# A recommender's interaction kernel: row fetches and product copies change engines, and the last tile is cut into four units

## The chip, the cores and the metric

The kernel runs on one core of one Trainium2 chip. The metric is the device time of one execution in microseconds (us), as a median over runs. All arithmetic is float32.

## The reference

2048 samples are scored. Each has 26 categorical fields; each field looks up a row of 64 numbers in its own table of 12,500 rows. A price gives one more vector of 64. All pairs of the 27 vectors are multiplied (351 products), and a small network follows:

```python
emb = emb_tables[jnp.arange(NUM_FIELDS)[:, None], x_cat]
emb = jnp.transpose(emb, (1, 0, 2))
dense_embed = price[:, None] @ Wp + bp
feats = jnp.concatenate([emb, dense_embed[:, None, :]], axis=1)
gram = jnp.einsum('bid,bjd->bij', feats, feats)
interactions = gram[:, _IU, _JU]
h = jax.nn.relu(dense_embed @ W1 + b1)
dense_out = jax.nn.relu(h @ W2 + b2)
concat = jnp.concatenate([interactions, dense_out], axis=1)
t = jax.nn.relu(concat @ Wt1 + bt1)
out = (t @ Wt2 + bt2)[:, 0]
```

## The kernel before

The samples are worked in 16 tiles of 128. For a tile GpSimd issues one indirect gather for each field (L251): 128 rows of 64 numbers, one for each partition, into `gathered`, of which there is one buffer. The fields stand in two chunks (0 to 13, 14 to 25). A chunk's gathers of the next tile wait until TensorE has transposed that chunk of this tile (`chunk_transposed`). Some columns are fetched without GpSimd: field 25 of nine tiles by SP and field 24 of five tiles by ScalarE, as 128 plain transfers of one row each (L171), whose addresses are first loaded into registers (L168), up to 32 at a time. They land in `pairs_of`, which has room for every such tile, so they can be issued far ahead. ScalarE issues its rows in portions that are written into its program: 26 after a tile's first chunk, 10 after the second and 8 between the two product rounds.

For each chunk TensorE transposes the fields in pairs into `ps_trans` (L500); VectorE copies the even fields and ScalarE the odd ones into `feats` (L196). The products of a tile are 32 matrix products of 128x128 in two rounds of 16 (L540; each is two instructions in the profile, so a round is 32). Both rounds write the same four banks of `ps_gram`, so round 2 waits until round 1 has been copied to `gram` (L186): 16 copies a round, 8 on VectorE and 8 on ScalarE. Tiles are put together into batches of 4, 4, 4, 2, 1 and 1. When a batch's last tile is done, its top layer (L563, L571: two sums of 1 + 7 products, `m` = 0 and 1), relus (ScalarE L339, VectorE L450), score (L579) and store (L344) are worked during the first tile of the next batch. Each engine works its program strictly in the order in which it is written; the waits are on semaphores.

The last tile (15) is laid out in another way: two units of 32 samples for each half of the partitions, with its gathers in four groups (8, 8, 8, 2 columns), four rounds of 8 products over alternating banks, and `keep_warm`, which puts dummy matmuls (L484) into TensorE's waits. Behind the last gather come one transpose, two rounds of products and copies, and the whole top layer of 128 columns.

Of the kernel before, what the change touches and what calls it, by code (L numbers as in the profile page):

```python
# [8 lines left out]
P = 128  # L9
# [6 lines left out]
UNITS = 2  # L16
UNIT = HALF // UNITS
# [9 lines left out]
LAST_CHUNKS = [(0, 8), (8, 16), (16, 24), (24, 26)]  # L27
LAST_ROUNDS = 4
LAST_RG = GROUPS // LAST_ROUNDS

BATCHES = [(0, 4), (4, 8), (8, 12), (12, 14), (14, 15), (15, 16)]
# [4 lines left out]
ACT_TILES = (3, 6, 9, 12, 14)  # L36
# [17 lines left out]
def rec_kernel(nc, price, x_cat, x_rows, table, consts, w1, w2, wt1_pairs, wt1_dense, out):  # L54
# [3 lines left out]
    with ExitStack() as ctx:  # L58
# [12 lines left out]
        last_base = sb("last_base", [P, FIELDS], i32)  # L71
# [65 lines left out]
        top_made = sem("top_made")  # L137
# [9 lines left out]
        last_from = ps_gram[:, :].rearrange("p (r h g s j c) -> p r h g s j c", r=2, h=2, g=LAST_RG, s=GROUP,  # L147
# [30 lines left out]

        def evacuate_gram(copy, t, r, quads):

            n = batch_of[t]
            rg = LAST_RG if t == LAST else RG
            source = last_from[:, r % 2] if t == LAST else gram_from
            for s in quads:
                for c in range(GROUP):
                    last = copy(gram_to[QUAD * c:QUAD * (c + 1), n % 2, t - BATCHES[n][0], :, rg * r:rg * (r + 1), :, s],  # L186
                                source[QUAD * s:QUAD * (s + 1), :, :, s, 0:SLABS, c])
            return last
# [45 lines left out]
        def _(pool):  # L234
# [439 lines left out]
```

## Time and profile before

| | |
|---|---|
| median of 3 runs | 525.37 us (524.44 to 528.44) |
| the profiled execution's own time | 526.02 us |
| its span | 524.1 us |
| GpSimd busy | 381.8 us, 73% of the span |
| TensorE busy (matmul) | 251.3 us, 48% |
| VectorE busy | 148.5 us, 28% |
| ScalarE busy, row fetches not counted | 165.6 us, 32% |
| mean granted TensorE clock | 0.697 of full speed |
| chain that ended last | GpSimd 62%, "issue" 24%, TensorE 5%, DMA 3% |

The issuing of transfers and the register loads are not counted as busy, so ScalarE, which issues 640 row transfers, is more occupied than its share says. A clock of 0.5 is 1.2 GHz and 1.0 is 2.4 GHz.

### The profile page before, as it was taken

Reading aid. Unit: us, or ns where it says so; the run is one execution under the profiler, and the core shown is the slowest. Engines: PE = TensorE matmul, PEld = TensorE weight load, DVE = VectorE, ACT = ScalarE, POOL = GpSimd, SP = SyncE. Lnnn points to the kernel's source line nnn. Section 1 sums busy time; section 2 is a strip of 40 time slices with the busy share of each in tenths; the row PEclk is TensorE's granted clock in tenths of the full one; section 3 lists DMA queues with packets and bytes.
Section 4 is the critical chain, followed back from the end, with each engine's and each line's share of the span. In section 5 each row is a group of like instructions: output and inputs, shape, how many; then the busy total and the mean of one; then the engine's idle time right before and its main releaser. Section 6 shows DMA issues by size and latency. Waiting matters only on the chain.

```text
span 524.1 us, 8045 instructions
## 1 busy us (share of the span) xinstructions
PE 251.3 (48%) x1496; PEld 183.4 (35%) x1496; DVE 148.5 (28%) x370; ACT 165.6 (32%) x405; POOL 381.8 (73%) x411
## 2 busy tenths in 40 slices
PE   0106234151469543443058772606246963467875
PEld 0105124051344323333053351605134333355764
DVE  6103304032240232314033132223324033143353
ACT  0023404133150342405024143332415016164463
POOL 6777777777777777777777777777777777777750
PEclk9999656565569766556566966665555888569798
DMA  6333333333333333233333333333332333332210
GB/s 192 27 28 29 28 29 27 29 28 28 28 29 27 29 28 30 28 28 28 28 30 27 28 29 28 29 29 29 27 29 28 27 30 28 28 29 26 28 22 2
DMA packets 17526, 16.50 MB, mean 31 GB/s; under 512 B 10530, under 2 KB 10786, under 8 KB 17347
## 3 DMA queue, kind: packets, MB, share of 16 engines
q0 software_dynamic: 12864, 13.20, 30.7%
q1 hardware_dynamic: 2884, 2.49, 1.5%
q10 hardware_dynamic: 1728, 0.30, 0.3%
q14 instruction: 38, 0.31, 0.2%
q8 instruction: 12, 0.20, 0.1%
HBM read 15.95 MB, written 0.01 MB: 30 GB/s over the span
## 4 chain that ended last, share of the span: by engine, by line
POOL 62%; issue 24%; PE 5%; DMA 3%; ACTq 2%; ACT 2%; DVE 0%; POOLq 0%
POOL gathered L251 61%; PE ps_mlp L571 3%; ACTq L171 2%; POOL pairs_of L251 2%; DMA gathered<-in_table,row_idx 2%; ACT gram L186 1%; PE ps_trans L500 1%; PE ps_gram L540 1%; DMA pairs_of<-in_table,row_idx 1%; PE ps_mlp L563 1%; ACTq L168 0%; DMA raw_idx<-in_x_cat 0%; POOLq L58 0%; ACT scores L344 0%; ACT top L339 0%
## 5 line engine op out<-in xcount | busy, mean ns | idle before, releaser
L251 POOL DMA_INDIRECT gathered<-in_table,row_idx x390 | 369.3, 947 | 120.4 <-issue 116.9
L540 PE MATMUL ps_gram<-feats 64*128 64x128 f32 x1024 | 111.9, 402 | 87.2 <-ACT gram L186 56.3
L540 PEld LDWEIGHTS ps_gram<-feats 64*128 64x128 f32 x1024 | 104.3, 306 | 101.5 <-issue 86.4
L186 DVE COPY gram<-ps_gram 32x112 f32<-32x112 f32 (+1 forms) x272 | 93.4, 343 | 152.8 <-PE ps_gram L540 149.6
L186 ACT COPY gram<-ps_gram 32x112 f32<-32x112 f32 (+1 forms) x272 | 93.7, 345 | 128.0 <-PE ps_gram L540 87.4
L500 PE MATMUL ps_trans<-ident,gathered 128*128 128x128 f32 x195 | 41.2, 368 | 173.9 <-DMA pairs_of<-in_table,row_idx 97.1
L500 PEld LDWEIGHTS ps_trans<-ident,gathered 128*128 128x128 f32 x195 | 31.0, 190 | 187.8 <-issue 186.3
L196 ACT COPY feats<-ps_trans 64x448 f32<-64x448 f32 (+1 forms) x60 | 34.1, 568 | 167.3 <-PE ps_trans L500 109.9
L196 DVE COPY feats<-ps_trans 64x448 f32<-64x448 f32 (+1 forms) x60 | 36.5, 609 | 148.9 <-PE ps_trans L500 148.3
L571 PE MATMUL ps_mlp<-gram,wt1p_sb 128*128 128x512 f32 (+2 forms) x168 | 60.8, 523 | 4.6 <-ACT gram L186 4.6
L571 PEld LDWEIGHTS ps_mlp<-gram,wt1p_sb 128*128 128x128 f32 x168 | 32.7, 229 | 33.7 <-issue 27.2
L450 DVE TENSOR_SCALAR top<-ps_mlp,consts_sb 128x512 f32<-128x512 f32 (+2 forms) x6 | 3.4, 573 | 65.4 <-PE ps_mlp L571 65.4
L289 ACT ACTIVATE feats<-price_bc,consts_sb 64x64 f32<-64x64 f32 x32 | 15.6, 488 | 0.7
L251 POOL DMA_INDIRECT pairs_of<-in_table,row_idx x12 | 11.3, 944 | 3.7 <-issue 3.7
L563 PE MATMUL ps_mlp<-dense_out,wt1d_sb 64*128 64x512 f32 (+2 forms) x24 | 12.5, 609 | 2.0 <-ACT dense_out L334 2.0
L339 ACT ACTIVATE top<-ps_mlp,consts_sb 128x512 f32<-128x512 f32 (+2 forms) x6 | 3.3, 545 | 26.2 <-PE ps_mlp L571 26.2
L196 ACT ACT_TABLE_LOAD x1 | 1.3, 1283 | 25.2 <-issue 25.2
L579 PE MATMUL ps_mlp<-top,consts_sb 128*1 128x512 f32 (+2 forms) x24 | 7.8, 449 | 1.0 <-DVE top L450 1.0
L530 PE MATMUL ps_mlp<-hidden,w_sb 128*64 128x512 f32 (+2 forms) x12 | 7.6, 728 | 0.5 <-ACT hidden L329 0.5
L563 PEld LDWEIGHTS ps_mlp<-dense_out,wt1d_sb 64*128 64x128 f32 x24 | 4.4, 227 | 6.3 <-issue 4.1
L525 PE MATMUL ps_mlp<-dense,w_sb 64*128 64x512 f32 (+2 forms) x12 | 5.8, 573 | 1.5 <-ACT scores L344 1.5
L484 PE MATMUL ps_trans<-wt1p_sb,ident 128*128 128x256 f32 x24 | 6.1, 389 | 0.0
(31 smaller groups left out, 52.4 us busy)
## 6 DMA issues: line engine op xcount, KB each, us to landing
pairs_of<-in_table SPq DMA_DIRECT2D x1152, 0.2 KB
pairs_of<-in_table ACTq DMA_DIRECT2D x640, 0.2 KB
gathered<-in_table,row_idx POOLq DMA_INDIRECT x390, 3.3
price_bc<-in_price SPq DMA_DIRECT2D x1, 1024.0 KB, 7.1
wt1p_sb<-in_wt_pairs SPq DMA_DIRECT2D x1, 896.0 KB, 9.2
raw_idx<-in_x_cat SPq DMA_DIRECT2D x1, 195.0 KB, 2.6
pairs_of<-in_table,row_idx POOLq DMA_INDIRECT x12, 3.3
w_sb<-in_w ACTq DMA_DIRECT2D x2, 32.0 KB, 4.0
```

The costliest lines, as they stand in the source:

```text
L171: eng.dma_start(field_at(t, f, 1)[p0 + k:p0 + k + 1, :].bitcast(u8), table_bytes[:, bass.ds(row, ROW_BYTES)])\
L186: last = copy(gram_to[QUAD * c:QUAD * (c + 1), n % 2, t - BATCHES[n][0], :, rg * r:rg * (r + 1), :, s], source[QUAD * s:QUAD * (s + 1), :, ...
L196: last = copy(feats[D * h:D * (h + 1), :, 1 + f0 + q:f1 + q:2], src[D * q:D * (q + 1), h, :, :])
L251: pool.indirect_dma_start(out=field_at(t, f, 1), out_offset=None, in_=rows, in_offset=bass.IndirectOffsetOnAxis(ap=row_idx[:, at:at + 1], ...
L289: return nc.scalar.activation(dst, price_bc[part, first:first + n], ACT.Identity, bias=const(BP, part), scale=const(WP, part))
L484: nc.tensor.matmul(ps_trans[:, BANK * bank:BANK * bank + TM1], ident[:, :], wt1p_sb[:, 0:TM1], start=True, stop=True)
L500: last = nc.tensor.transpose(ps_trans[:, to + k * P:to + (k + 1) * P], field_at(t, f, 2), ident[:, :])
L530: nc.tensor.matmul(ps_mlp[1][0:BM2, 0:width(n)], w2_sb[:, :], hidden[:, 0:width(n)], start=True, stop=True)\
L540: last = nc.tensor.matmul(ps_gram[:, out_at:out_at + P], group, group, start=True, stop=True)
L563: nc.tensor.matmul(ps_mlp[m][:, 0:w], wt1d_sb[:, m * P:(m + 1) * P], dense_out[:, 0:w], start=True, stop=False)
L571: last = nc.tensor.matmul(ps_mlp[m][:, 0:w], wt1p_sb[:, j * TM1 + m * P:j * TM1 + (m + 1) * P], gram[:, at:at + w], start=False, stop=(j = ...
L579: last = nc.tensor.matmul(ps_mlp[0][0:1, 0:width(n)], const(WT2 + m), top[m][:, 0:width(n)], start=(m == 0), stop=(m == 1))
```

## The change

ScalarE now fetches field 24 of seven tiles row by row instead of five (896 rows, in portions of 28 and 36 for each tile). For that, the product copies of tiles 0 to 13 are all VectorE's, 16 a round. The small network of the price (`hidden_layer`, `dense_out_layer`) is worked in the first four tiles for all samples. The batches are 4, 4, 4, 2 and 2 tiles, so the top layer of tile 14 is not worked alone. Tile 14's products go in four rounds of 8 over alternating banks, and both engines copy them.

The last tile is gathered in four units of 32 samples (7, 6, 7 and 6 columns); each unit has its own transposes, copies and one round of 8 products. The top layer of the last batch is split: 160 columns (tile 14 and unit 0) are summed around unit 1's products, the other 96 (units 1 to 3) at the end, in `ps_trans`. The output leaves in two transfers, all but the last 96 scores first. The row indices of the last tile are made by twelve small adds on VectorE instead of one. The dummy matmuls are now four before unit 3's transposes and four before the late top sums.

```diff
-UNITS = 2
-UNIT = HALF // UNITS
+UNITS = 4
+UNIT = P // UNITS
...
-BATCHES = [(0, 4), (4, 8), (8, 12), (12, 14), (14, 15), (15, 16)]
+BATCHES = [(0, 4), (4, 8), (8, 12), (12, 14), (14, 16)]
...
-ACT_TILES = (3, 6, 9, 12, 14)
+ACT_TILES = (2, 4, 6, 8, 10, 12, 14)
...
-FIRST_ROWS, AFTER_FIRST_CHUNK, AFTER_CHUNKS, BETWEEN_ROUNDS = 24, 26, 10, 8
+FIRST_ROWS, AFTER_FIRST_CHUNK, AFTER_CHUNKS = 24, 28, 36
...
-WARM = (0, 7, 3, 1, 1)
-TO_GRAM, TO_TOP = 4, 5
+WARM = (0, 0, 4, 4)
...
+            for late in range(2):
+                part = slice(BATCH - LATE, BATCH) if late else slice(0, BATCH - LATE)
+                sp.wait_ge(score_stored, len(BATCHES) + late)
+                sp.dma_start(out.rearrange("(o b) -> o b", o=1)[:, part], scores[:, part]).then_inc(out_written, 16)
...
             def gram_round(r, t):
-                dve.wait_ge(gram_done, ROUNDS * t + r + 1)
-                evacuate_gram(nc.vector.tensor_copy, t, r, (0, 1)).then_inc(gram_evac_dve, 1)
+                dve.wait_ge(gram_done, rounds_before(t) + r + 1)
+                evacuate_gram(nc.vector.tensor_copy, t, r, range(GROUP) if t < LAST - 1 else (0, 1)).then_inc(gram_evac_dve, 1)
...
-            t, n = LAST, batch_of[LAST]
-            even_last(0)
-            top_relu(n - 1)
-            even_last(1)
-            for r in range(LAST_ROUNDS // 2):
-                gram_round(r, t)
-            even_last(2)
-            even_last(3)
-            for r in range(LAST_ROUNDS // 2, LAST_ROUNDS):
-                gram_round(r, t)
-            top_relu(n)
+            t = LAST
+            for n in range(UNITS):
+                even_unit(n)
+                gram_round(n, t)
+                if n == 1:
+                    part_relu(0)
+            part_relu(1)
...
+            for n in range(UNITS):
+                transpose_unit(n)
+                if n == 1:
+                    top_part(0, 0)
+                fine_round(LAST, n)
+                if n == 1:
+                    top_part(1, 0)
+                if n == 2:
+                    score_part(0)
+            keep_warm(UNITS, 0)
+            for m in range(2):
+                top_part(m, 1)
+            score_part(1)
```

ScalarE's program from the top relu of the batch of tiles 8 to 11, in tile 12. `pairs_of<-in_table` are the row fetches, `x26` that many of them. Before:

```order
L339 ACTIVATE top<-ps_mlp,consts_sb 128x512 [waits top_summed0]
L168 TENSOR_LOAD by_row_at
L171 DMA pairs_of<-in_table 1x256 x26
L196 COPY feats<-ps_trans 64x64x6 [waits chunk_transposed1]
L196 COPY feats<-ps_trans 64x64x6
L344 ACTIVATE scores<-ps_mlp,consts_sb 1x512 [waits score_summed]
L168 TENSOR_LOAD by_row_at
L171 DMA pairs_of<-in_table 1x256 x10
L186 COPY gram<-ps_gram 32x2x8x7 [waits gram_done]
L186 COPY gram<-ps_gram 32x2x8x7 x7
```

And now:

```order
L368 ACTIVATE top<-ps_mlp,consts_sb 128x512 [waits top_summed0]
L175 TENSOR_LOAD by_row_at
L178 DMA pairs_of<-in_table 1x256 x28
L212 COPY feats<-ps_trans 64x64x6 [waits chunk_transposed1]
L212 COPY feats<-ps_trans 64x64x6
L378 ACTIVATE scores<-ps_mlp,consts_sb 1x512 [waits score_summed]
L175 TENSOR_LOAD by_row_at
L178 DMA pairs_of<-in_table 1x256 x32
L175 TENSOR_LOAD by_row_at
L178 DMA pairs_of<-in_table 1x256 x4
```

The 16 product copies of the tile are gone, and the fetches that stood around them follow the second chunk's copies in one piece of 32 + 4 rows; the portion behind the top relu has grown from 26 to 28 rows, with the odd copies of the second chunk still behind it.

VectorE's program in tile 13, before:

```order
L196 COPY feats<-ps_trans 64x64x7 [waits chunk_transposed0]
L196 COPY feats<-ps_trans 64x64x7
L196 COPY feats<-ps_trans 64x64x6 [waits chunk_transposed1]
L196 COPY feats<-ps_trans 64x64x6
L186 COPY gram<-ps_gram 32x2x8x7 [waits gram_done]
L186 COPY gram<-ps_gram 32x2x8x7 x7
L186 COPY gram<-ps_gram 32x2x8x7 [waits gram_done]
L186 COPY gram<-ps_gram 32x2x8x7 x7
```

And now:

```order
L212 COPY feats<-ps_trans 64x64x7 [waits chunk_transposed0]
L212 COPY feats<-ps_trans 64x64x7
L212 COPY feats<-ps_trans 64x64x6 [waits chunk_transposed1]
L212 COPY feats<-ps_trans 64x64x6
L203 COPY gram<-ps_gram 32x2x8x7 [waits gram_done]
L203 COPY gram<-ps_gram 32x2x8x7 x15
L203 COPY gram<-ps_gram 32x2x8x7 [waits gram_done]
L203 COPY gram<-ps_gram 32x2x8x7 x15
```

Each round has 16 copies for 8; the second round of products, which writes the same banks, can only follow the sixteenth copy.

TensorE's end, from the dummies before the last group's transposes. Before:

```order
L484 MATMUL ps_trans<-wt1p_sb,ident 128x256 [waits trans_evac_act,trans_evac_dve]
L484 MATMUL ps_trans<-wt1p_sb,ident 128x256 x2
L500 MATMUL ps_trans<-ident,gathered 128x128 [waits last_gathered3]
L484 MATMUL ps_trans<-wt1p_sb,ident 128x256 [waits trans_evac_act,trans_evac_dve]
L540 MATMUL ps_gram<-feats 128x128 [waits gram_evac_dve,dense_slot_set,gram_evac_act,trans_evac_act,trans_evac_dve]
L540 MATMUL ps_gram<-feats 128x128 x7
L540 MATMUL ps_gram<-feats 128x128 [waits gram_evac_dve,dense_slot_set,gram_evac_act,trans_evac_act,trans_evac_dve]
L540 MATMUL ps_gram<-feats 128x128 x7
L563 MATMUL ps_mlp<-dense_out,wt1d_sb 128x128 [waits dense_out_made]
L484 MATMUL ps_trans<-wt1p_sb,ident 128x256
L571 MATMUL ps_mlp<-gram,wt1p_sb 128x128 [waits gram_evac_act,gram_evac_dve]
```

And now:

```order
L536 MATMUL ps_trans<-wt1p_sb,ident 128x256 [waits trans_evac_act,trans_evac_dve]
L536 MATMUL ps_trans<-wt1p_sb,ident 128x256 x3
L574 MATMUL ps_trans<-ident,gathered 128x128 [waits unit_gathered3]
L574 MATMUL ps_trans<-ident,gathered 128x128 x2
L621 MATMUL ps_gram<-feats 128x128 [waits gram_evac_dve,dense_slot_set,gram_evac_act,trans_evac_act,trans_evac_dve]
L621 MATMUL ps_gram<-feats 128x128 x7
L536 MATMUL ps_trans<-wt1p_sb,ident 128x256 x4
L627 MATMUL ps_trans<-dense_out,wt1d_sb 128x96
L632 MATMUL ps_trans<-gram,wt1p_sb 128x96 [waits gram_evac_act,gram_evac_dve]
L632 MATMUL ps_trans<-gram,wt1p_sb 128x96 x6
L627 MATMUL ps_trans<-dense_out,wt1d_sb 128x96
L632 MATMUL ps_trans<-gram,wt1p_sb 128x96 [waits gram_evac_act,gram_evac_dve]
```

One round of products stands behind the last transposes instead of two, and the top sums behind it are 96 columns wide instead of 128.

## Rows read from the trace of the kernel before

**Rows 1.** Page part 5: costliest groups of instructions, GpSimd's gathers.

```profile
L251 POOL DMA_INDIRECT gathered<-in_table,row_idx x390 | 369.3, 947 | 120.4 <-issue 116.9
...
L251 POOL DMA_INDIRECT pairs_of<-in_table,row_idx x12 | 11.3, 944 | 3.7 <-issue 3.7
```

**Rows 2.** Timeline of the tail (start us, us, engine line op names shapes xcount [idle before]).

```profile
505.90 0.94 POOL L251 DMA_INDIRECT gathered<-in_table,row_idx  x1 [0.31 <-issue]
...
508.71 0.33 PE L500 MATMUL ps_trans<-ident,gathered 128*128 128x128 f32 x1 [0.60 <-DMA gathered<-in_table,row_idx]
...
509.72 2.06 PE L540 MATMUL ps_gram<-feats 64*128 64x128 f32 x32 [0.24 <-DVE feats L211]
...
510.92 4.29 DVE L186 COPY gram<-ps_gram 32x56 f32<-32x56 f32 x16 [1.30 <-PE ps_gram L540]
...
515.36 2.83 PE L571 MATMUL ps_mlp<-gram,wt1p_sb 128*128 128x128 f32 x14 [2.76 <-ACT gram L186]
...
518.83 2.04 PE L571 MATMUL ps_mlp<-gram,wt1p_sb 128*128 128x128 f32 x14
...
521.96 0.36 ACT L344 ACTIVATE scores<-ps_mlp,consts_sb 1x128 f32<-1x128 f32 x1 [3.37 <-PE ps_mlp L579]
```

**Rows 3.** Timeline of ScalarE, tile 7 at 247, tile 12 from 414, tile 13 at 452.

```profile
247.29 1.26 ACT L196 COPY feats<-ps_trans 64x448 f32<-64x448 f32 x2 [1.67 <-PE ps_trans L500]
...
249.51 8.59 ACTq L171 DMA_DIRECT2D pairs_of<-in_table  x26
...
414.17 0.69 ACT L339 ACTIVATE top<-ps_mlp,consts_sb 128x512 f32<-128x512 f32 x1 [7.59 <-PE ps_mlp L571]
...
425.48 1.03 ACT L196 COPY feats<-ps_trans 64x384 f32<-64x384 f32 x2 [10.62 <-issue]
...
428.00 3.45 ACTq L171 DMA_DIRECT2D pairs_of<-in_table  x10
...
452.18 1.03 ACT L196 COPY feats<-ps_trans 64x384 f32<-64x384 f32 x2 [8.38 <-issue]
```

**Rows 4.** Timeline of VectorE and GpSimd in the opening, and one gather at 392.

```profile
6.99 0.18 DVE L428 TENSOR_TENSOR row_idx<-clamped,last_base 128x26 uint32<-128x26 f32 x1
...
9.53 1.42 POOL L251 DMA_INDIRECT gathered<-in_table,row_idx  x1 [0.30 <-issue]
...
392.27 0.94 POOL L251 DMA_INDIRECT gathered<-in_table,row_idx  x1 [0.31 <-issue]
```

**Rows 5.** SP's timeline; and line 168, register loads, ns min/median/max.

```profile
7.40 457.20 SPq L171 DMA_DIRECT2D pairs_of<-in_table  x1152
...
L168 ACTq TENSOR_LOAD <-by_row_at x47: 483/2094/2430, 15.1 to 459.3; - x47
```

**Rows 6.** Timeline of VectorE and TensorE, second chunk and products of tile 11.

```profile
386.30 1.21 DVE L196 COPY feats<-ps_trans 64x384 f32<-64x384 f32 x2 [12.56 <-PE ps_trans L500]
...
387.56 3.78 PE L540 MATMUL ps_gram<-feats 64*128 64x128 f32 x32 [1.30 <-DVE feats L196]
...
391.39 2.84 DVE L186 COPY gram<-ps_gram 32x112 f32<-32x112 f32 x8 [3.88 <-PE ps_gram L540]
```

**Rows 7.** Timeline of TensorE's top sums in tiles 12 and 14, VectorE's copies then.

```profile
405.67 8.45 PE L571 MATMUL ps_mlp<-gram,wt1p_sb 128*128 128x512 f32 x14
...
468.28 4.86 PE L571 MATMUL ps_mlp<-gram,wt1p_sb 128*128 128x256 f32 x14 [1.81 <-ACT gram L186]
...
473.70 3.29 PE L571 MATMUL ps_mlp<-gram,wt1p_sb 128*128 128x256 f32 x14
...
477.77 1.21 DVE L196 COPY feats<-ps_trans 64x384 f32<-64x384 f32 x2 [0.26 <-PE ps_trans L500]
```

**Rows 8.** Groups by line and shape, window 464 to 530, VectorE's copies.

```profile
L186 DVE COPY gram<-ps_gram 32x56 f32<-32x56 f32 x32 | 8.2, 255 | 4.8 <-PE ps_gram L540 4.3
...
L211 DVE COPY feats<-ps_trans 64x192 f32<-64x192 f32 x2 | 1.0, 484 | 0.1
```

**Rows 9.** TensorE by stretch: us, busy (xcount), granted clock, DMA share, GB/s.

```profile
515.00:518.00 3.00, 2.65 (x14) 0.65 0.00 0
```

More of the change, by code:

```diff
@@ L15 @@
 HALF = P // 2
-UNITS = 2
-UNIT = HALF // UNITS
+UNITS = 4
+UNIT = P // UNITS
+SIDE = UNIT // 2
+COLS = FIELDS // UNITS
+SHARED = UNITS * COLS
 GROUPS = HALF // GROUP
@@ L136, in rec_kernel @@
         top_summed = [sem(f"top_summed{m}") for m in range(2)]
-        top_made = sem("top_made")
+        top_made = [sem(f"top_made{m}") for m in range(2)]
         score_summed = sem("score_summed")
@@ new lines, in top_sums @@
+            def top_sums(n, m, part, to, rounds):
+                a, first = BATCHES[n][0] * P, (n % 2) * SLABS * WIDE * P
+                nc.tensor.matmul(to, wt1d_sb[:, m * P:(m + 1) * P], dense_out[:, a + part.start:a + part.stop],
+                                 start=True, stop=False)
+                wait_gram_evac(rounds)
+                for j in range(SLABS):
+                    at = first + j * WIDE * P
+                    last = nc.tensor.matmul(to, wt1p_sb[:, j * TM1 + m * P:j * TM1 + (m + 1) * P],
+                                            gram[:, at + part.start:at + part.stop], start=False, stop=(j == SLABS - 1))
+                last.then_inc(top_summed[m], 1)
@@ L575, in score, with top_part @@
+            def top_part(m, late):
+                if not late:
+                    pe.wait_ge(score_stored, last_batch)
+                top_sums(last_batch, m, *last_part(m, late), rounds_before(LAST) + (FINE_ROUNDS if late else 1))
             def score(n):
-                pe.wait_ge(top_made, 2 * n + 2)
                 for m in range(2):
+                    pe.wait_ge(top_made[m], n + 1)
                     last = nc.tensor.matmul(ps_mlp[0][0:1, 0:width(n)], const(WT2 + m), top[m][:, 0:width(n)],
+                                            start=(m == 0), stop=(m == 1))
+                last.then_inc(score_summed, 1)
@@ L580, in score, with score_part @@
+            def score_part(late):
+                part, _ = last_part(0, late)
+                for m in range(2):
+                    pe.wait_ge(top_made[m], last_batch + 1 + late)
+                    last = nc.tensor.matmul(ps_mlp[late][0:1, 0:part.stop - part.start], const(WT2 + m), top[m][:, part],
                                             start=(m == 0), stop=(m == 1))
@@ L651 @@
     idx = cat.transpose(2, 1, 0).copy()
-    idx[:, -1] = cat[:, -1].reshape(FIELDS // 2, 2, 2, UNITS, UNIT).transpose(1, 2, 4, 3, 0).reshape(P, FIELDS)
+    last = cat[:, -1].reshape(FIELDS, UNITS, 2, SIDE)
+    own = last[:SHARED].reshape(COLS, UNITS, UNITS, 2, SIDE).transpose(1, 3, 4, 2, 0).reshape(P, UNITS, COLS)
+    shared = last[SHARED:].reshape(2, 2, 2, 2, SIDE).transpose(2, 0, 3, 4, 1).reshape(P, 2)
+    for n in range(UNITS):
+        idx[:, -1, UNIT_COLS[n][0]:UNIT_COLS[n][0] + COLS] = own[:, n]
+        if n % 2 == 0:
+            idx[:, -1, UNIT_COLS[n][COLS]] = shared[:, n // 2]
     idx = idx.reshape(P, TILES * FIELDS)
```

344 lines of the change are left out of this document (191 added, 153 removed).

## Prediction

> **What bounds the kernel now.** I read the page's costliest groups first. GpSimd issues 390 + 12 = 402 gathers of 0.94 us with 0.30 us between them, almost nothing of it a wait for another engine [rows 1]: one gather every 1.25 us, up to the last one at 505.90 us. Behind it stands a tail of 18.2 us to the span's end at 524.1: landing 2.8 us, transposes, copies, products, 4.29 us of product copies, the two top sums, score, store and the output [rows 2]. So there are two ways to gain: fewer gathers, or a shorter tail. Everything else has been hidden, and I then read how well: the timeline of the three compute engines around tiles 11 to 14, and ScalarE's row fetches in it.
>
> There the cover is thin. ScalarE does its row fetches between its copies, and the copies wait behind them: at tile 12 it takes the top sum at 414.17 and reaches the odd copies of the second chunk only at 425.48, and those of tile 13 at 452.18 [rows 3]. TensorE's products wait for these copies.
>
> **The change, part by part.** *Gathers.* 16 of 416 columns are fetched row by row instead of 14: 400 gathers, 2 x 1.25 = 2.5 us earlier at the end (by tile 11 both are already gone, so tiles 11 to 15 arrive 2.5 us earlier).
>
> *Opening.* Twelve small adds on VectorE take the place of one of 0.18 us, and its row addresses are 14% longer; beside such work a gather takes up to 1.42 us instead of 0.94, 0.34 us lost for each us of it [rows 4]. With some 2.3 us more of it the bounds are 0 and 0.8 us; I take 0.35, since most opening gathers lose less than that slowest one. Last gather: 505.90 - 2.5 + 0.35 = 503.8.
>
> *ScalarE.* It loses 16 product copies per tile and gets 28 + 36 rows per tile for 26 + 10 + 8. From the start of its copies to the end of 26 rows it needs (249.51 + 8.59) - 247.29 = 10.8 us [rows 3]; 28 rows: 11.5. SP, whose 1152 rows are 36 pieces of 32, needs 457.2 / 36 = 12.7 us for each [rows 5]; the 36 are a piece of 32 and one of 4, 12.7 + 2.1 (0.48 for the shortest register load, 4 x 0.34, gaps) = 14.8; with the gaps a tile costs ScalarE about 26.9 us. A tile is 24 to 26 gathers, 30 to 32.5 us. It fits, but in a batch's first tile ScalarE first waits for the top sum and then fetches 28 rows.
>
> *VectorE.* 16 copies of 0.355 us instead of 8 beside ScalarE: 5.7 us a round for 2.84 to 3.2, with ScalarE no longer late for the round. TensorE's second round waits for it, so a tile's products take 2 x (3.8 + 5.7) = 19 us [rows 6].
>
> Now the path. Tile 8 is a batch's first tile like tile 12, 100 gathers or 125 us ahead of it: its odd copies start near 425.5 - 125 = 300.5 now, and about then after the change (two rows more, but an earlier arrival); three tiles of 26.9 bring ScalarE to tile 11's at 381.2, before the transposes, 386.30 - 2.5 = 383.8 [rows 6]. Products: 383.8 + 1.3 + 3.8 + 5.7 + 3.9 + 5.7 = 404.2. Top sum of tiles 8 to 11: 8.45 [rows 7], to 412.8. ScalarE to the odd copies of tile 12: 11.3 + 0.7 = 12.0, to 424.8. From there 14.8 of rows, or products 1.1 + 3.4 + 5.7 + 3.5 and the next transposes, 1.3: both about 440. 28 rows: 451.5, tile 13's odd copies. That is where they are now (452.18), though the gathers came 2.5 us earlier: **the two saved gathers are gone in ScalarE's queue.** Products and copies of tile 13: 1.1 + 3.9 + 5.7 + 3.8 + 5.7, to 471.7, where the top sum now starts at 468.28: VectorE's longer copies cost another 3.5 us. First sum 5.3 (4.86 now, 6.0 wholly at 1.2 GHz), second 0.6 + 3.3, transposes 0.9: tile 14's last copies start at 481.9 instead of 477.77 [rows 7].
>
> *Last tiles*, with the shapes of [rows 2] and [rows 8]. Tile 14 in four rounds: 1.3 + 1.2, then 4 x 2.15 (half of 4.29) of copies on both engines: 493.0. Unit 0: dense slots 1.0, copies 1.0, products 1.3, copies 2.15: 498.4. Unit 1 and the early top sums: 160 columns are not in the trace; 14 instructions lie between 2.04 (128 columns) and 3.29 (256), I take 2.3. First sum 500.9, products 502.2, second sum 504.9. Unit 2: transposes 0.7, VectorE two copies of the shared columns (64 elements; 56 take 0.26) and two of 0.48, 1.5, products 1.3: 508.4, copied at 510.5; TensorE does the score and four dummies (8 instructions of 256 columns at 3.29 / 14 = 0.235 [rows 7], 1.9) to 510.9. Unit 3, landed since 503.8 + 2.8 = 506.6: transposes 511.5, copies 512.5, products 513.8, copied 515.9, first late sum (96 columns; at most 2.04, at least three quarters of it, 1.5; take 1.8) 517.9, second 520.2, relu, score, store 521.4, output 1.8: 523.2. TensorE is idle in half of this stretch. Its granted clock fell to 0.65 on average in the stretch after the last wait of now [rows 9], and fourteen instructions took 2.83 instead of 2.04 [rows 2]; I add 2.0 (bounds 0 and 4). **Span 525.2, 1.1 more than 524.1.**
>
> The Trainium skill speaks against this change here (TensorE: Matmul & The Clock Gate, "HAM oscillation"): short bursts of matmuls with idle time between them fall back to the half clock each time. By that rule the end would stand at the bound of 4 us, a span of 527.2, and by [rows 9], where part of such a stretch ran at full clock, at 2.
>
> The profiled execution has 526.02 us for its span of 524.1, 0.65 above the median of three. I apply the difference to the median: 525.37 + 1.1 = **526.5 us**.
>
> **Rivals.** *Nothing is late.* ScalarE is through its rows before each second chunk, and unit 3 is taken when it lands: transposes 507.2 instead of 511.5, 4.3 less, and the clock's 2.0 shrinks to 1: span 519.9 to 518.9, time 520.1 to 521.1. For it: the tail alone is really shorter, one round of copies behind the last gather instead of two (2.15), 96 columns for 128, and the output of the rest already gone. Against it: ScalarE at 452.18 today, with 8 rows fewer a tile 13. Chance 0.14. This is about the most that the change can give: 1%.
>
> *ScalarE does not catch up* (the other side). The 10 rows behind the second chunk's copies come 2.5 us after these started (425.48 to 428.00 [rows 3]), as late as 26 rows behind their copies (247.29 to 249.51), though the shortest load takes 0.48 [rows 5]; if the 36 carry such a surcharge, or a row takes 0.36, a tile costs 28.8. It decides from (383.8 - 300.5) / 3 = 27.8 us a tile: above it ScalarE is still late at tile 12, and again at 13. At 28.8: 3 us late at tile 8, 5.4 at tile 11, 7.5 at tile 13's odd copies, and TensorE's transposes then hold up GpSimd too (their slack is eleven gathers, 13.7 us, less some 5 for landing and transposes). Span 525.2 + 7.5 = 532.7, time 534. Chance 0.16.
>
> *VectorE's copying slows the gathers.* At the opening's 0.34 us for each us, 28 rounds x 2.84 = 80 us more copying would cost up to 27 us, a span of 552. But the gather at 392.27, beside the product copies that began at 391.39, takes 0.94 us [rows 4, 6]. Chance 0.02. The Trainium skill (SBUF — State Buffer, "Who interferes with whom") says why both can be: a VectorE instruction with two SBUF inputs holds up a GpSimd one that reads SBUF, and fp32 copies from SBUF to SBUF starve the gathers, but with one SBUF input at most and outside the two-port modes there is no contention; by its warning on copies alone this change would be slower, by its condition not, and the trace agrees with the condition.
>
> **How the numbers follow.** Forecast 0.63 (524 to 529), nothing late 0.14 (half of it just beyond 1%), ScalarE late 0.16, gathers slowed 0.02; the other 0.05 are smaller mishaps within 1%. A measurement of this kernel tells about 1% from no change, 520.1 and 530.6: faster 0.09, within 0.73, slower 0.18. Range 520.5 to 532, which leaves half of the first rival and most of the slow ones out. The forecast's own range is 524 to 529.
>
> **What would show it.** 400 gathers every 1.25 us, the last started near 503.8. ScalarE's odd copies of tile 13 near 451 and its rows ending just before; gaps of TensorE in front of them. The top sum of tiles 12 and 13 starting near 472. Unit 3's transposes near 511 rather than 507; if they stand at 507, the chain through ScalarE was not late. A GpSimd wait on transposes around tiles 9, 13 or 14 would show the slow rival. A gather over 1.0 us in mid-kernel would show shared ports.

## The result and the profile after

The changed kernel takes 529.2 us (median of 20 runs, 527.0 to 531.3), the kernel before 526.18 us (20 runs, 524.44 to 528.53): ratio 1.0057, 95% interval 1.0043 to 1.0071, 0.6% slower. The forecast was 526.5 us against 525.37, a ratio of 1.0022, most likely within 1%. The profiled execution of the changed kernel has 530.84 us and a span of 528.9 us, that of before 526.02 and 524.1. The spans below stand 1.8 to 2.1 us under the times; the profiled execution after is at the upper end of its runs.

GpSimd in the page's costliest groups, then the slowest gather of the opening, the two gathers ahead of which it waits for TensorE, and the last one (start us, us, engine line op names xcount [idle before]); they answer to [rows 1, 2]:

```profile
L274 POOL DMA_INDIRECT gathered<-in_table,row_idx x394 | 373.9, 949 | 124.3 <-issue 118.4
```

```profile
12.60 1.56 POOL L274 DMA_INDIRECT gathered<-in_table,row_idx  x1 [0.30 <-issue]
...
195.09 0.94 POOL L274 DMA_INDIRECT gathered<-in_table,row_idx  x1 [0.94 <-PE ps_trans L553]
...
321.56 0.94 POOL L274 DMA_INDIRECT gathered<-in_table,row_idx  x1 [1.85 <-PE ps_trans L553]
...
506.36 0.94 POOL L274 DMA_INDIRECT gathered<-in_table,row_idx  x1 [0.30 <-issue]
```

Two gathers are gone, 2.5 us, and yet the last one starts at 506.36, later than the 505.90 of [rows 2]. Eight slow gathers of the opening cost 2.06 us over 0.95 where seven cost 1.31 before, 0.75 more; the slowest of them, 1.56 us, is slower than the 1.42 of [rows 4]. The two waits cost 0.64 and 1.55 us beyond the usual 0.30. 505.90 - 2.5 + 0.75 + 2.19 = 506.34.

ScalarE's timeline in tiles 12 and 13, for [rows 3]:

```profile
416.77 0.69 ACT L368 ACTIVATE top<-ps_mlp,consts_sb 128x512 f32<-128x512 f32 x1 [9.97 <-PE ps_mlp L632]
419.04 9.38 ACTq L178 DMA_DIRECT2D pairs_of<-in_table  x28
428.47 1.03 ACT L212 COPY feats<-ps_trans 64x384 f32<-64x384 f32 x2 [11.01 <-issue]
...
430.79 13.10 ACTq L178 DMA_DIRECT2D pairs_of<-in_table  x36
...
446.17 9.58 ACTq L178 DMA_DIRECT2D pairs_of<-in_table  x28
455.79 1.03 ACT L212 COPY feats<-ps_trans 64x384 f32<-64x384 f32 x2 [9.33 <-issue]
```

The odd copies of the second chunk come at 428.47 in tile 12 (425.48 before) and at 455.79 in tile 13 (452.18 before), each time the moment the 28 rows are issued. The chain that ended last shows who waited (start us, us, what; "issue" is a wait that it can't put down to an engine). In the kernel before, this chain ran along the gathers up to 505.90 [rows 2]; now it leaves them in tile 11:

```profile
381.49 3.85 DMA pairs_of<-in_table,row_idx
385.58 1.53 PE ps_trans L553 x6
388.70 3.80 PE ps_gram L600 x32
398.42 3.80 PE ps_gram L600 x32
408.07 8.66 PE ps_mlp L632 x14
...
426.45 3.15 issue
429.60 3.49 PE ps_gram L600 x32
439.01 3.80 PE ps_gram L600 x32
449.96 1.55 PE ps_trans L553 x6
452.72 4.20 issue
456.92 3.80 PE ps_gram L600 x32
466.64 3.80 PE ps_gram L600 x32
476.30 5.68 PE ps_mlp L632 x14
```

The two "issue" pieces, 3.15 and 4.20 us, are TensorE waiting with the transposes done, until ScalarE is through its rows. VectorE's sixteen copies lie between the rounds:

```profile
392.52 5.75 DVE L203 COPY gram<-ps_gram 32x112 f32<-32x112 f32 x16 [4.21 <-PE ps_gram L600]
```

5.75 us, twice the 2.84 of [rows 6]. The top sum of tiles 12 and 13 starts at 476.30, where [rows 7] has 468.28. TensorE's timeline of the last tile, for [rows 2]:

```profile
499.62 2.08 PE L621 MATMUL ps_gram<-feats 64*128 64x128 f32 x16 [4.30 <-ACT feats L222]
...
503.97 4.07 PE L632 MATMUL ps_mlp<-gram,wt1p_sb 128*128 128x160 f32 x14 [0.61 <-DVE gram L198]
...
509.56 2.17 PE L632 MATMUL ps_mlp<-gram,wt1p_sb 128*128 128x160 f32 x14
...
513.75 1.16 PE L621 MATMUL ps_gram<-feats 64*128 64x128 f32 x16 [1.59 <-DVE feats L222]
...
517.31 0.49 PE L574 MATMUL ps_trans<-ident,gathered 128*128 128x128 f32 x3
...
522.45 1.77 PE L632 MATMUL ps_trans<-gram,wt1p_sb 128*128 128x96 f32 x14
...
524.54 1.80 PE L632 MATMUL ps_trans<-gram,wt1p_sb 128*128 128x96 f32 x14
```

Unit 3's transposes begin at 517.31. Its last gather started at 506.36 and landed near 509, so they come 8 us later than they could: no work of this tail waits for GpSimd any more. The clock by stretch (us, TensorE busy, granted clock, DMA share, GB/s), for [rows 9]:

```profile
500.00:508.00 8.00, 7.39 (x37) 0.50 0.14 27
...
515.00:518.00 3.00, 2.80 (x15) 1.00 0.00 0
520.00:528.00 8.00, 6.86 (x46) 1.00 0.01 2
```

### The profile page after: what moved, and what is told of

Read it like the earlier page. It is cut to its first block, busy times and chain, and to the rows that moved or that the text cites. A ratio compares the mean times of both kernels' runs of the same rounds, so it can differ in the third digit from the quotient of the medians.

```text
span 528.9 us, 8560 instructions
## 1 busy us (share of the span) xinstructions
PE 252.3 (48%) x1481; PEld 184.7 (35%) x1481; DVE 229.1 (43%) x623; ACT 86.5 (16%) x189; POOL 380.3 (72%) x407
## 4 chain that ended last, share of the span: by engine, by line
POOL 34%; PE 28%; issue 18%; DVE 15%; DMA 3%; ACT 2%; POOLq 0%
POOL gathered L274 34%; DVE gram L203 13%; PE ps_mlp L632 11%; PE ps_gram L600 9%; PE ps_trans L553 2%; DMA pairs_of<-in_table,row_idx 2%; ACT gram L200 2%; DVE feats L212 1%; PE ps_gram L621 1%; PE ps_mlp L653 1%; DMA gathered<-in_table,row_idx 1%; PE ps_mlp L627 1%; PE ps_trans L536 1%; PE ps_trans L632 1%; DVE gram L198 0%
## 5 line engine op out<-in xcount | busy, mean ns | idle before, releaser
L274 POOL DMA_INDIRECT gathered<-in_table,row_idx x394 | 373.9, 949 | 124.3 <-issue 118.4
L203 DVE COPY gram<-ps_gram 32x112 f32<-32x112 f32 x448 | 155.8, 348 | 146.3 <-PE ps_gram L600 136.7
L600 PE MATMUL ps_gram<-feats 64*128 64x128 f32 x896 | 104.6, 419 | 121.8 <-DVE gram L203 83.1
L553 PE MATMUL ps_trans<-ident,gathered 128*128 128x128 f32 x184 | 38.7, 369 | 131.5 <-DMA gathered<-in_table,row_idx 70.3
L500 DVE TENSOR_SCALAR top<-ps_mlp,consts_sb 128x512 f32<-128x512 f32 (+1 forms) x4 | 2.7, 684 | 52.3 <-PE ps_mlp L632 52.3
L621 PE MATMUL ps_gram<-feats 64*128 64x128 f32 x128 | 10.2, 305 | 9.9 <-ACT feats L222 4.3
L198 DVE COPY gram<-ps_gram 32x56 f32<-32x56 f32 x32 | 8.2, 257 | 10.2 <-PE ps_gram L621 9.9
L363 ACT ACTIVATE dense_out<-ps_mlp,consts_sb 64x512 f32<-64x512 f32 x4 | 2.7, 682 | 59.0 <-PE ps_mlp L590 29.6
L198 ACT COPY gram<-ps_gram 32x56 f32<-32x56 f32 x32 | 8.3, 259 | 6.6 <-PE ps_gram L621 6.2
L200 DVE COPY gram<-ps_gram 32x56 f32<-32x56 f32 x32 | 8.0, 251 | 1.7 <-PE ps_gram L621 1.3
L368 ACT ACTIVATE top<-ps_mlp,consts_sb 128x512 f32<-128x512 f32 (+1 forms) x4 | 2.5, 634 | 36.5 <-PE ps_mlp L632 36.5
L200 ACT COPY gram<-ps_gram 32x56 f32<-32x56 f32 x32 | 8.1, 253 | 1.4 <-PE ps_gram L621 1.0
L584 PE MATMUL ps_mlp<-dense,w_sb 64*128 64x512 f32 x8 | 8.3, 1137 | 0.0
```

The source lines that it names most:

```text
L198: last = copy(gram_unit[to, w, k, r, :, :, :, s], fine_from[part, r % 2, :, :, s, 0:SLABS, c])
L200: last = copy(gram_to[to, w, k, :, FINE_RG * r:FINE_RG * (r + 1), :, s], fine_from[part, r % 2, :, :, s, 0:SLABS, c])
L203: last = copy(gram_to[to, w, k, :, RG * r:RG * (r + 1), :, s], gram_from[part, :, :, s, 0:SLABS, c])
L274: pool.indirect_dma_start(out=field_at(t, f, 1), out_offset=None, in_=rows, in_offset=bass.IndirectOffsetOnAxis(ap=row_idx[:, at:at + 1], ...
L553: last = nc.tensor.transpose(ps_trans[:, to + k * P:to + (k + 1) * P], field_at(t, f, 2), ident[:, :])
L584: nc.tensor.matmul(ps_mlp[0][:, :], w1_sb[:, :], dense[:, :], start=True, stop=True).then_inc(hidden_summed, 1)
```

## The experiments

Twelve runs of seven kernels. Each edit is made in the changed kernel. The runs fell on five chips, always beside the kernel before, so ratios are compared, and spans only with care. On two of the chips every kernel, the one before too, takes at least 340 us more; what these runs can say stands at the end of this section. The theory was that ScalarE's queue sets the pace in tiles 12 and 13; the rivals were VectorE's long rounds and the last tile's own work.

**The old tiles 0 to 13 under the new last tiles.** The product copies are shared again, and ScalarE fetches five tiles in the old portions.

```diff
-ACT_TILES = (2, 4, 6, 8, 10, 12, 14)
+ACT_TILES = (3, 6, 9, 12, 14)
...
-FIRST_ROWS, AFTER_FIRST_CHUNK, AFTER_CHUNKS = 24, 28, 36
+FIRST_ROWS, AFTER_FIRST_CHUNK, AFTER_CHUNKS, BETWEEN_ROUNDS = 24, 26, 10, 8
...
-                evacuate_gram(nc.vector.tensor_copy, t, r, range(GROUP) if t < LAST - 1 else (0, 1)).then_inc(gram_evac_dve, 1)
+                evacuate_gram(nc.vector.tensor_copy, t, r, (0, 1)).then_inc(gram_evac_dve, 1)
```

> The changed kernel's last two tiles, opening, batches and dense network, but with tiles 0 to 13 as before: product copies split 8 and 8 between the engines, ScalarE fetches five tiles in portions of 24, 26, 10 and 8 rows, 402 gathers. Theory (tiles 0 to 13 lose the time, the last tile in units gains some): last gather 505.90 + 0.75 of the opening = 506.7, top sum of tiles 12 and 13 near 468, tile 14's last copies near 478, unit 3's transposes right behind its landing, about 510.5, and from there the 11.6 us of the changed kernel (517.31 to 528.9): span about 522, ratio to the kernel before about 0.996. Rival (the units themselves cost more than the old tail): span 526 or more, ratio above 1.003.

Measured: 523.89 us beside 527.07, ratio 0.9938 (0.9915 to 0.996), span 522.7; the last gather started at 507.26, and TensorE's timeline has

```profile
468.43 4.95 PE L635 MATMUL ps_mlp<-gram,wt1p_sb 128*128 128x256 f32 x14 [1.17 <-ACT gram L203]
...
511.02 0.49 PE L577 MATMUL ps_trans<-ident,gathered 128*128 128x128 f32 x3
```

As the theory had it (468, 510.5, 522). The rest of the change taken together (the last two tiles, the early top sums, the batches, the network in the first four tiles) is a gain of 0.6%; the run doesn't part these from one another. The last gather is 1.36 us behind the 505.90 of [rows 2], but not for the reason expected: six slow gathers of this opening cost 1.38 us over 0.95, hardly more than before, and the gathers of this run start 1.2515 us apart instead of 1.2487. The changed tiles 0 to 13 turn the gain into a loss: 1.0057 - 0.9938 = 0.0119, 6.3 us.

**Five tiles for ScalarE instead of seven, VectorE still copying alone.** This cuts those 6.3 us in two.

```diff
-ACT_TILES = (2, 4, 6, 8, 10, 12, 14)
+ACT_TILES = (3, 6, 9, 12, 14)
...
-FIRST_ROWS, AFTER_FIRST_CHUNK, AFTER_CHUNKS = 24, 28, 36
+FIRST_ROWS, AFTER_FIRST_CHUNK, AFTER_CHUNKS = 24, 20, 24
```

> The changed kernel, but ScalarE fetches five tiles instead of seven (3, 6, 9, 12, 14) in portions of 24, 20 and 24 rows: 402 gathers, 44 rows a tile instead of 64; all product copies of tiles 0 to 13 stay VectorE's. Against the kernel with the old tiles 0 to 13 (span 522.7, five tiles too, copies split 8 and 8) it shows what VectorE's sixteen copies cost, against the changed kernel (528.9) what the two more tiles cost. Theory (most of the loss is ScalarE's rows): 20 rows behind the top relu, odd copies of tile 12 near 424; second chunk of tile 13 at its transposes near 449.5, products 3.8 + 5.75 + 3.8 + 5.75, top sum near 470 instead of 468.43 (old tiles) and 476.30 (changed kernel); span about 524.3, ratio to the kernel before 0.997. Rival (VectorE's long rounds are the loss): top sum at 474 or later, span 527 or more, ratio 1.003 or more.

Measured: 523.43 us beside 526.12, ratio 0.9952 (0.9933 to 0.997), span 521.7. ScalarE in tiles 12 and 13, and TensorE's top sum:

```profile
424.16 1.03 ACT L212 COPY feats<-ps_trans 64x384 f32<-64x384 f32 x2 [7.58 <-PE ps_trans L553]
...
448.68 1.03 ACT L212 COPY feats<-ps_trans 64x384 f32<-64x384 f32 x2 [7.37 <-PE ps_trans L553]
```

```profile
469.10 5.51 PE L632 MATMUL ps_mlp<-gram,wt1p_sb 128*128 128x256 f32 x14 [2.82 <-DVE gram L203]
```

Both odd copies now wait for transposes and not for rows, and the top sum comes at 469.10, 0.7 us behind the kernel with shared copies, whose gathers were late by themselves (the last one at 507.26, here at 506.13). So with five tiles VectorE's sixteen copies cost 0.9952 - 0.9938 = 0.0014, less than the intervals; beside these copies the two more tiles of rows cost 1.0057 - 0.9952 = 0.0105, 5.5 us, although they save two gathers. This settles it between rows and rounds. Seven tiles with shared copies were not run, so what the long rounds add once ScalarE is late isn't shown.

**The rows in another place.** Nothing is left out: in the tiles 4, 8, 12 and 14 the 28 rows are issued while ScalarE would wait for the top sum, and not behind it.

```diff
+                fetch_some(AFTER_FIRST_CHUNK)
                 if first:
                     top_relu(n - 1)
-                fetch_some(AFTER_FIRST_CHUNK)
                 odd_fields(1, t)
```

> The changed kernel with one edit: in the tiles 4, 8, 12 and 14 ScalarE issues the 28 rows ahead of the top relu, in the 10 us in which it now waits for the top sum (406.8 to 416.77 in tile 12), instead of behind it. Theory (the end is set by a chain through ScalarE's queue): the odd copies of tile 12's second chunk come at about 425 instead of 428.47, right behind TensorE's transposes (424.6); the two waits of GpSimd at 195 and 321 (0.94 and 1.85 us) vanish, last gather near 504.2; the chain from tile 12 on shifts by 3.6 us: span about 525.3 instead of 528.9, ratio to the kernel before about 0.999. Rival (VectorE's doubled copies, not the rows, hold the chain): the odd copies move, the products do not start earlier, ratio stays 1.006.

Measured: 524.5 us beside 525.46, ratio 0.9981 (0.9965 to 0.9997), span 523.2, with

```profile
413.99 0.69 ACT L368 ACTIVATE top<-ps_mlp,consts_sb 128x512 f32<-128x512 f32 x1 [9.53 <-PE ps_mlp L632]
421.90 1.03 ACT L212 COPY feats<-ps_trans 64x384 f32<-64x384 f32 x2 [7.22 <-PE ps_trans L553]
```

No gather waits for TensorE beyond the usual 0.30 us any more, and the last one starts at 504.18 (504.2 was expected). The shift was undersized: the odd copies of tile 12 come 6.6 us earlier, 3.8 of it between the top relu and them (7.9 instead of 11.7), and 2.8 because the top relu itself comes earlier; 2.2 of these are the gathers' two waits. One line of order is worth 1.0057 - 0.9981 = 0.0076, 4.0 us. The tail is still late: in tile 13 the odd copies wait for 28 rows until 450.54, and unit 3's transposes come at 511.53, over 7 us behind the start of the last gather.

**Rows ahead, none in tile 13, and tile 13's copies shared.** Beside the edit above:

```diff
-                fetch_some(AFTER_CHUNKS)
-                if t == LAST - 1:
-                    for r in range(FINE_ROUNDS):
+                fetch_some(AFTER_CHUNKS + (4 if t < 10 else 0))
+                if t >= LAST - 2:
+                    for r in range(ROUNDS if t < LAST - 1 else FINE_ROUNDS):
...
-                evacuate_gram(nc.vector.tensor_copy, t, r, range(GROUP) if t < LAST - 1 else (0, 1)).then_inc(gram_evac_dve, 1)
+                evacuate_gram(nc.vector.tensor_copy, t, r, range(GROUP) if t < LAST - 2 else (0, 1)).then_inc(gram_evac_dve, 1)
```

> The changed kernel with three edits in ScalarE's and VectorE's programs: the 28 rows ahead of the top relu in the tiles 4, 8, 12 and 14; 40 rows instead of 36 behind the second chunk of tiles 0 to 9, so that tile 13 has none; and the product copies of tile 13 shared by both engines, 8 and 8. 400 gathers as before. Theory (the change's loss lies in the rows and long copies of tiles 12 and 13 alone): odd copies of tile 12 near 425, of tile 13 near 448 instead of 455.79, top sum of tiles 12 and 13 at 463 to 465 instead of 476.30, tile 14's last copies near 475, last gather near 504.2, unit 3's transposes right behind its landing near 507.2, then 11.7 us: span about 519, ratio to the kernel before about 0.987. Rival (the gathers of tile 14 are held up by transposes elsewhere, or four rows more a tile make ScalarE late from the first tiles): span 522.7 or more, no better than the kernel with the old tiles 0 to 13.

Measured: 520.44 us beside 525.46, ratio 0.9913 (0.9886 to 0.994), span 518.4. TensorE's timeline:

```profile
465.41 5.09 PE L632 MATMUL ps_mlp<-gram,wt1p_sb 128*128 128x256 f32 x14
...
506.65 0.55 PE L574 MATMUL ps_trans<-ident,gathered 128*128 128x128 f32 x3 [1.21 <-DMA gathered<-in_table,row_idx]
```

The last transposes wait for the landing again, 2.5 us behind the last gather's start at 504.13, and from there it is 11.75 us to the end. This is faster than both kernels, by 0.9% against the one before, and it is the prediction's rival "nothing is late" (518.9 to 519.9) brought about. Against the kernel with the rows ahead it gains 0.9981 - 0.9913 = 0.0068, 3.6 us; how much of this is the rows that tile 13 no longer has, and how much its shared copies, was not measured.

**The dummies and the clock.** These runs fell on the two slow chips, whose times don't compare; but their last 20 us, in which no row is fetched, have the same durations as elsewhere: from the start of unit 2's products to the end of the span the changed kernel needs 528.9 - 513.75 = 15.15 us, and the kernel with the rows ahead on such a chip 868.8 - 853.65 = 15.15. That stretch is compared.

```diff
-WARM = (0, 0, 4, 4)
+WARM = (0, 0, 0, 4)
```

> The changed kernel without the four dummy products ahead of unit 3's transposes (1.99 us from 515.48), where unit 3 has landed long before. Theory (they lie on the path now that TensorE is late, and only pay if the clock would fall without them): transposes 1.8 us earlier, unit 3's products at most 0.9 us longer (1.16 against 2.08), the last dummies stay: span 0.9 to 1.8 us shorter. Rival (the granted clock falls for the late top sums too): the two sums and products take 1.88 times as long, 3.9 us more, span 2 us longer.

Measured: ratio 1.0051 (1.0025 to 1.0077); the stretch is 867.5 - 851.01 = 16.5 us, 1.3 us longer. The transposes came at once:

```profile
852.74 0.55 PE L574 MATMUL ps_trans<-ident,gathered 128*128 128x128 f32 x3
855.96 1.83 PE L621 MATMUL ps_gram<-feats 64*128 64x128 f32 x16 [2.67 <-DVE feats L222]
857.72 2.95 PE L536 MATMUL ps_trans<-wt1p_sb,ident 128*128 128x256 f32 x8
```

ScalarE's timeline at the same place:

```profile
852.22 2.24 ACT L198 COPY gram<-ps_gram 32x56 f32<-32x56 f32 x8 [1.79 <-PE ps_gram L621]
...
854.89 0.97 ACT L222 COPY feats<-ps_trans 64x192 f32<-64x192 f32 x2
```

The theory, a gain of 0.9 to 1.8 us, failed in two points. The four dummies are hardly on the path: ScalarE copies unit 2's products until 854.46 and takes unit 3's features only then, so the 1.8 us gained on TensorE become 0.2 at unit 3's products (4.95 us behind the start of unit 2's instead of 5.16). And without them the products (1.83 for 1.16) and the next dummies (2.95 for 1.99) run in part at the half clock. The late sums did not (1.80 each), which the rival had wanted.

In the kernel "late tiles", all dummies away, `WARM = (0, 0, 0, 0)`:

> The kernel with ScalarE's rows ahead of the top relu, none in tile 13 and that tile's product copies shared (span 518.4, unit 3's transposes right behind their landing at 506.65), now without the eight dummy products, which there lie wholly beside waits for the landing and for the last product copies. Theory (the dummies hold the granted clock at 1.0 in the last stretch): unit 3's products 2.08 instead of 1.16 us, the two late sums 3.3 each instead of 1.77 and 1.80, their two first products 0.9 longer: span 3 to 4.8 us longer, 521.4 to 523.2. Rival (unit 2's and unit 3's own work holds the clock): span within 0.5 us of 518.4.

Measured: ratio 1.0171 (1.014 to 1.0202), and in the stretch

```profile
877.41 3.27 PE L632 MATMUL ps_trans<-gram,wt1p_sb 128*128 128x96 f32 x14 [2.08 <-DVE gram L198]
...
881.28 3.30 PE L632 MATMUL ps_trans<-gram,wt1p_sb 128*128 128x96 f32 x14
```

887.3 - 868.41 = 18.9 us, 3.7 more than with the dummies; the granted clock from 872 to 887 was 0.56, against 1.00 in the kernel with the rows ahead from 854 to 868. The eight dummies are worth 3.7 us at this end, as the theory had it (3 to 4.8); by the run above, 1.3 of them are those of the first four. The rest of the ratio, about 9 us over the others there, lies ahead of this stretch; the kernel "late tiles" with its dummies was not run on that chip, so its cause stays open.

Eight dummies more between unit 0's transposes and products, in the idle time of 4.3 us there:

```diff
-WARM = (0, 0, 4, 4)
+WARM = (8, 0, 4, 4)
...
-                keep_warm(n, n % 2)
+                if n > 1:
+                    keep_warm(n, n % 2)
...
+                if n == 0:
+                    keep_warm(1, 1)
```

> The changed kernel with eight dummy products more, on TensorE between unit 0's transposes and its products, where it is idle from 495.3 to 499.6 (4.3 us; four of them take 1.99 us at 1.0). Theory (the half clock in unit 0's products and the first early top sum costs time on the path): the products take 1.16 instead of 2.08 us, the fourteen instructions of 160 columns 2.2 instead of 4.07, span 2.0 to 2.8 us shorter, about 526.5. Rival (the chain behind it is set by the copies, or the dummies run at half clock and delay the products): no change, or up to 4 us longer.

The second run had the same expectation, the third one more number:

> The changed kernel with eight dummy products more, on TensorE between unit 0's transposes and its products, where it is idle from 495.3 to 499.6 (4.3 us; four of them take 1.99 us at 1.0). Theory (the half clock in unit 0's products and the first early top sum costs time on the path): the products take 1.16 instead of 2.08 us, the fourteen instructions of 160 columns 2.2 instead of 4.07, span 2.0 to 2.8 us shorter, about 526.5. Rival (the chain behind it is set by the copies, or the dummies run at half clock and delay the products): no change, or up to 4 us longer.

> The changed kernel with eight dummy products more, on TensorE between unit 0's transposes and its products, where it is idle from 495.3 to 499.6 (4.3 us; four of them take 1.99 us at 1.0). Theory (the half clock in unit 0's products and the first early top sum costs time on the path): the products take 1.16 instead of 2.08 us, the fourteen instructions of 160 columns 2.2 instead of 4.07, and the stretch from the start of unit 0's products to that of unit 2's 11.2 us instead of 14.13; span 2.0 to 2.8 us shorter, about 526.5. Rival (the chain behind it is set by the copies, or the dummies run at half clock and delay the products): no change, or up to 4 us longer.

It ran three times, each time on a slow chip: ratios 1.0014 (0.999 to 1.0038), 1.0026 (0.9996 to 1.0055) and 1.003 (1.0002 to 1.0058). From the start of unit 0's products to unit 2's it took 13.97, 11.17 and 13.64 us, against 14.13 in the changed kernel. In the second the products and the first early sum ran at the high level:

```profile
839.11 4.43 PE L536 MATMUL ps_trans<-wt1p_sb,ident 128*128 128x256 f32 x10 [0.60 <-issue]
845.52 1.16 PE L622 MATMUL ps_gram<-feats 64*128 64x128 f32 x16 [1.98 <-ACT feats L222]
...
849.06 2.14 PE L633 MATMUL ps_mlp<-gram,wt1p_sb 128*128 128x160 f32 x14 [1.44 <-ACT gram L198]
```

The dummies did not hold the clock there: it was granted at 0.50 from 839 to 843.5, so they ran at the half level themselves, and at 1.00 from 845.5 on. In the other two runs the products took 2.08 us, at 0.50. In the third the dummies were as long (ten instructions in 4.57 us at 0.50), with 3.44 us of idle time behind them in place of 1.98, and the clock did not rise. In the first the clock was 1.00 from 829 to 832, 0.59 beside the last five dummy instructions, and 0.50 in the 3.75 us of idle time behind them. So the half clock costs 14.13 - 11.17 = 3.0 us in this stretch. These dummies removed it in one run of three, and why in that one stays open. None of the three shows what eight would do in the 4.3 us of the other chips: here TensorE had over 12 us between unit 0's transposes and its products, and the dummies lay scattered in them.

**The slow chips.** The first runs of the kernels with the old tiles, with the rows ahead and with five tiles fell on them. Their expectations were those of the second runs, but for the rival of the rows ahead:

> The changed kernel's last two tiles, opening, batches and dense network, but with tiles 0 to 13 as before: product copies split 8 and 8 between the engines, ScalarE fetches five tiles in portions of 24, 26, 10 and 8 rows, 402 gathers. Theory (tiles 0 to 13 lose the time, the last tile in units gains some): last gather 505.90 + 0.75 of the opening = 506.7, top sum of tiles 12 and 13 near 468, tile 14's last copies near 478, unit 3's transposes right behind its landing, about 510.5, and from there the 11.6 us of the changed kernel (517.31 to 528.9): span about 522, ratio to the kernel before about 0.996. Rival (the units themselves cost more than the old tail): span 526 or more, ratio above 1.003.

> The changed kernel with one edit: in the tiles 4, 8, 12 and 14 ScalarE issues the 28 rows ahead of the top relu, in the 10 us in which it now waits for the top sum (406.8 to 416.77 in tile 12), instead of behind it. Theory (the end is set by a chain through ScalarE's queue): the odd copies of tile 12's second chunk come at about 425 instead of 428.47, right behind TensorE's transposes (424.6); the two waits of GpSimd at 195 and 321 (0.94 and 1.85 us) vanish, last gather near 504.2; the chain from tile 12 on shifts by 3.6 us: span about 525.3 instead of 528.9, ratio to the kernel before about 0.999. Rival (the last tile's own work is too long, whatever comes ahead of it): the odd copies move, the end does not, ratio stays 1.006.

> The changed kernel, but ScalarE fetches five tiles instead of seven (3, 6, 9, 12, 14) in portions of 24, 20 and 24 rows: 402 gathers, 44 rows a tile instead of 64; all product copies of tiles 0 to 13 stay VectorE's. Against the kernel with the old tiles 0 to 13 (span 522.7, five tiles too, copies split 8 and 8) it shows what VectorE's sixteen copies cost, against the changed kernel (528.9) what the two more tiles cost. Theory (most of the loss is ScalarE's rows): 20 rows behind the top relu, odd copies of tile 12 near 424; second chunk of tile 13 at its transposes near 449.5, products 3.8 + 5.75 + 3.8 + 5.75, top sum near 470 instead of 468.43 (old tiles) and 476.30 (changed kernel); span about 524.3, ratio to the kernel before 0.997. Rival (VectorE's long rounds are the loss): top sum at 474 or later, span 527 or more, ratio 1.003 or more.

None of the forecast places can be read there, since the ends are set elsewhere. Measured: 866.82 us (ratio 0.9987, 0.9963 to 1.0011), 870.3 (1.0053, 1.0027 to 1.0079) and 875.4 (1.001, 0.9989 to 1.0032), beside 866.37, 866.37 and 874.88 for the kernel before. SP's and ScalarE's timelines of the first:

```profile
7.41 800.73 SPq L178 DMA_DIRECT2D pairs_of<-in_table  x1152
```

```profile
399.54 24.56 ACTq L178 DMA_DIRECT2D pairs_of<-in_table  x13
```

SP's 1152 transfers take 800.73 us there, 457.20 in [rows 5], and thirteen of ScalarE's 24.56 us instead of some 5. The chain that ended last is 60% SP's queue, so GpSimd's gathers, which bound the kernel elsewhere, don't there.

## Why the prediction held, and where it was off

By its own steps, in the spans of the two profiled executions:

| Step | forecast | measured |
|---|---|---|
| last gather starts | 503.8 | 506.36 |
| products of tile 11 start | 385.1 | 388.70 |
| odd copies, second chunk of tile 12 | 424.8 | 428.47 |
| the same of tile 13 | 451.5 | 455.79 |
| top sum of tiles 12 and 13 starts | 471.7 | 476.30 |
| tile 14's last feature copies | 481.9 | 486.51 |
| unit 0's copies start | 493.0 | 497.52 |
| first early sum ends | 500.9 | 508.04 |
| unit 3's transposes end | 511.5 | 517.80 |
| end of the span | 525.2 | 528.9 |

**Right: the mechanism and the sign of the tail.** The two saved gathers are gone in ScalarE's queue; the odd copies of tile 13 wait for its 28 rows; the last transposes come long after their landing; VectorE's round takes 5.75 us (5.7 forecast) and slows no gather in mid-kernel. The run with five tiles shows that the rows are the main cause, and the one with the rows ahead that their place is. From tile 11 to tile 14 the forecast's intervals hold within 0.6 us: 39.7 from tile 11's products to tile 12's odd copies (39.8 measured), 26.7 to tile 13's (27.3), 20.2 to the top sum (20.5), 10.2 to tile 14's copies (10.2), 11.1 to the units (11.0).

**Off: the arrival.** The step "its odd copies start near 300.5 now, and about then after the change" failed. Before the change they do (300.16); after it they come at 305.14:

```profile
284.21 9.14 PE L632 MATMUL ps_mlp<-gram,wt1p_sb 128*128 128x512 f32 x14 [1.30 <-DVE gram L203]
...
305.14 1.03 ACT L212 COPY feats<-ps_trans 64x384 f32<-64x384 f32 x2 [11.06 <-issue]
```

Of these 5.0 us, 2.0 are there before the top sum: TensorE transposes tile 8's first chunk at 279.19 instead of 277.20. The sum then waited 1.30 us for VectorE's copies of tile 7 (the forecast counted the long rounds in tile 11, but not there), and it took 9.14 us for 7.71, at a granted clock of 0.68 for 0.81. The 28 rows that follow the relu add only 0.2 to what 26 took; but they stand behind it, so its lateness reaches the copies in full. Behind the batches' first tiles, 4 and 8, TensorE's first transposes of tiles 5 and 9 came so late that the gathers of tiles 6 and 10, which wait for them, stood 0.64 and 1.55 us. That the rows behind the relu are their cause is shown by the run with the rows ahead, which has neither wait. The forecast had this only in its rival "ScalarE does not catch up", at 0.16 and with 7.5 us. What happened is a light form of it: late in the batches' first tiles, caught up by the fourth (in tile 11 ScalarE ends its rows 0.4 us behind the transposes), and the 2.2 us stayed in the gathers. The opening cost 0.75 us instead of 0.35, because the slowest gather beside VectorE was not the one of [rows 4]; and the forecast left its 0.35 out where it put tile 11's transposes at 386.30 - 2.5. Together this is 2.9 of the 3.6 us by which tile 11's products are late. The last gather of tile 11 took 0.4 us longer to the transposes (4.09 from its start for 3.71), and the odd copies began at 387.57, 0.4 us behind VectorE's at 387.13.

**Off: where the clock falls.** The forecast put 2.0 us for the half clock behind unit 2, by [rows 9]. It fell earlier, in unit 0's products and the first early sum: 2.08 and 4.07 us for the 1.3 and 2.3 taken, 2.6 us, and none behind unit 2, where the granted clock is 1.00 and the dummies hold it. The sizes came to nearly the same, the place did not. The Trainium skill's rule (TensorE: Matmul & The Clock Gate, "HAM oscillation") is that short bursts of matmuls with idle time between them fall back to the half clock. By the prediction's own reading it would have brought 4 us. The run without dummies (3.7 us) and the 3.0 us in units 0 and 1 agree with it; the end of the changed kernel doesn't test it, since dummies fill the idle time there.

**Off: the end.** From the end of unit 3's transposes it took 11.1 us for a forecast of 13.7, which had the 2.0 of the clock in it. This error hid a part of the others: the changed kernel was 3.6 us late at tile 11's products, 4.5 at unit 0, 7.1 at the end of the first early sum, 6.3 at these transposes, and 3.7 at the end. That the time came so near is in part luck.

The time of the profiled execution exceeds the median by 1.6 us. By medians the miss is 1.0057 against 1.0022, 1.8 us.

## What to carry to other kernels

Transfers that an engine issues belong to the chain of whoever needs that engine next, so they go into a wait that is there anyway: here one such move was worth 4.0 us, more than the 2.5 of the two gathers that the transfers replaced. Follow a slower piece through every batch and not only through the last one, since what it delays early (here the gathers behind tiles 5 and 9) was never given back. A shorter tail pays only as long as it still begins with the arrival of its data; look whether its first instruction waits for the landing.

## What the runs showed of the hardware

- The same program takes 526 us on some chips and 866 to 875 on two others, by the pace at which SP and ScalarE issue row transfers (SP's 1152 in 457 to 460 us and in 801 to 819). The trace shows longer intervals between the transfers, with no engine or semaphore that they wait for; the cause stays open. A kernel that hangs on many small issued transfers should be timed on more than one chip.
- The same dummies ahead of the same products left these at the high level in one run (1.16 us) and at the half in two (2.08 us). In the first of these cases the dummies themselves ran at the half level, and the clock rose behind them.
- VectorE copying the products of tiles 0 to 13 alone, 155.8 us of copies, left the gathers of the middle at 0.94 us.
